# Adding the last attention norm's ln_beta to the residual rows in the first graph layer, in a late VectorE stage

## The reference, cut to what matters

```python
x = _layernorm(x + _L0_gnn_ref(x, edge_index, ...))                 # first layer: graph convolution
x = _layernorm(x + _L1_gnn_ref(x, edge_index, edge_weight1, ...))   # second layer: attention, 3 rounds
x = _layernorm(x + _L2_gnn_ref(...))
x = _layernorm(x + _L3_gnn_ref(...))

def _L1_gnn_ref(x, ...):
    x = _layer_norm(x, ln_in_g, ln_in_b)
    for l in range(3):
        h = elu(_transformer_conv(x, ...))
        x = _layer_norm(x + h, ln_g[l], ln_b[l])   # (x - mu) * rsqrt(var + eps) * g + b
    return x
```

## Time and profile before

| what | value |
|---|---|
| median of 3 runs | 7026.21 us (7023.27 to 7031.01) |
| the profiled execution's own time | 7027.23 us |
| its span in the profile | 7025.3 us |
| VectorE busy | 5733.4 us (82%) |
| TensorE busy | 4875.6 us (69%) |
| ScalarE busy | 4768.1 us (68%) |
| GpSimd busy | 4470.3 us (64%) |
| mean granted TensorE clock | 0.84 |

### The profile page before, as it was taken

The page is one execution under the profiler, slowest core; times in us unless marked ns, Lnnn a source line. Parts: engine busy times, 40 slices in busy tenths (PEclk is TensorE's granted clock), DMA queues, the critical chain, the costliest instruction groups (busy, mean ns, idle before and its releaser), DMA issues. The chain is left out here.

```text
span 7025.3 us, 129182 instructions
## 1 busy us (share of the span) xinstructions
PE 4875.6 (69%) x27083; PEld 3611.4 (51%) x27083; DVE 5733.4 (82%) x28646; ACT 4768.1 (68%) x13748; POOL 4470.3 (64%) x4380
## 2 busy tenths in 40 slices
PE   4104333332999987999948888884997659888882
PEld 1002222221877766777736666653664547666661
DVE  9814777775999987999949999995775877999996
ACT  0002888884888885888948888883553656888884
POOL 7776777772655526555537777744774445777774
PEclk8555555555999998999979999996998989999995
DMA  3333555552555534555524555544664873444441
GB/s 100 99 104 83 133 131 128 130 132 84 178 185 178 190 138 140 185 185 177 176 86 152 170 170 170 169 147 130 205 203 148 295 269 120 148 147 147 147 145 44
DMA packets 507778, 1065.66 MB, mean 152 GB/s; under 512 B 225329, under 2 KB 259196, under 8 KB 506998
## 3 DMA queue, kind: packets, MB, share of 16 engines
q1 hardware_dynamic: 373618, 811.78, 35.3%
q0 software_dynamic: 133504, 247.46, 13.2%
HBM read 559.18 MB, written 500.53 MB: 151 GB/s over the span
## 5 line engine op out<-in xcount | busy, mean ns | idle before, releaser
L1801 POOL DMA_INDIRECT xs<-tab,rec x1176 | 1187.9, 1010 | 737.0 <-issue 325.1
L1891 ACT ACTIVATE z<-p_a 128x512 f32<-128x512 f32 x1176 | 696.4, 592 | 307.1 <-PE p_a L1734 299.3
L1885 ACT ACTIVATE st<-xs,cb 128x128 f32<-128x128 f32 x2352 | 807.5, 395 | 0.5 <-DVE cg L1530 0.5
L1836 PE MATMUL p_a<-w_all,xt 128*128 128x256 f32 x2352 | 735.5, 395 | 19.9 <-ACT xt L1876 16.4
L1804 POOL DMA_INDIRECT xd<-tab,rec x616 | 621.0, 1008 | 187.8 <-issue 179.9
L1839 PE MATMUL p_y<-w_all,xt 128*128 128x258 f32 x2352 | 725.0, 390 | 21.1 <-DVE cA L1956 20.5
L1991 DVE SCALAR_TENSOR_TENSOR st<-st,cg 128x128 f32<-128x128 f32 x2352 | 711.5, 342 | 6.8 <-ACT st L1885 4.6
L1956 DVE CUSTOM_DVE_ANT_0 junk<-p_y,xs 128x129 f32<-128x129 f32 x2352 | 579.9, 283 | 53.5 <-PE p_y L1839 51.1
L1738 PE MATMUL p_m<-w_all,z 128*128 128x128 f32 x2352 | 580.0, 329 | 0.0
L999 PE MATMUL p_m<-b_rows,ones_bf 3*128 3x512 bf16 x224 | 100.1, 447 | 688.8 <-ACT z L1042 688.8
L1734 PE MATMUL p_a<-ident,st 128*128 128x128 f32 x2352 | 465.2, 280 | 145.1 <-DVE st L1991 144.9
(11 more groups left out here) (756 smaller groups left out, 16246.7 us busy)
## 6 DMA issues: line engine op xcount, KB each, us to landing
states<-st SPq DMA_DIRECT2D x168, 910.0 KB
own<-tab SPq DMA_DIRECT2D x168, 448.0 KB
tab<-o SPq DMA_DIRECT2D x168, 448.0 KB
runs<-run SPq DMA_DIRECT2D x112, 448.0 KB, 2.9
tab<-out SPq DMA_DIRECT2D x112, 448.0 KB
x<-tab SPq DMA_DIRECT2D x112, 448.0 KB, 4.3
angles<-st SPq DMA_DIRECT2D x56, 532.0 KB, 2.9
xsrc<-got SPq DMA_DIRECT2D x56, 448.0 KB
```

The costliest lines, as they stand in the source:

```text
L1801: pool.indirect_dma_start(xs[:, i, j, 0:D], None, table, bass.IndirectOffsetOnAxis(ap=rec[:, i, SRC, j : j + 1], axis=0)).then_inc(got_in[ ...
L1836: ins = pe.matmul(p_a[two(own_c, own_i)][:, 2 * D : 4 * D], xt[:, two(c, i), D : 2 * D], k.w_own[:], start=True, stop=True)
L1885: ins = act.activation(state_of(r, j)[:, h, :], xs[:, c.slot(UB), j, 0:D], ACT.Copy, scale=co.b[:, c.slot(2), h, j : j + 1])
L1891: act.activation(z[:, c.slot(RING), j, :], p_a[two(c, j)][:], ACT.Copy).then_inc(st_copied, 1)
```

## The change

The vector `ln_b[2]` is no longer added in the third attention round. The first layer adds it to the residual rows before they are stored, in a new VectorE stage `lift` with lag -3, the last one of the list. The stores of chunk n-3 wait for `lifted` and no longer for `second.applied2`; the loads still wait for `finished`. The vector is loaded once, ahead of SyncE's first load, into `last_b`. In `conv` the addition goes, and the addition of `res` stays at j = 2.

```diff
-        self.finished = sem("finished")
+        self.finished, self.storable = sem("finished"), None
...
                     c = chunk(t, u, -DRAIN)
                     if c.there:
-                        wait(sp, self.finished, c.count(1, 1), self.passed)
+                        wait(sp, self.storable or self.finished, c.count(1, 1), self.passed)
                         for i, table in enumerate(outs):
...
+        last_b, lifted, b_in = sb("last_b", [P, D]), sem("lifted"), sem("b_in")
...
+        def lift(dve, step, c):
+
+            dve.wait_ge(second.applied2, c.count(1, 1))
+            dve.tensor_tensor(R(n.o[0], c), R(n.o[0], c), every(last_b), ALU.add).then_inc(lifted, 1)
+
+        def bring_b(sp):
+            sp.dma_start(last_b[:], A["L1_gnn_ln_b"][k.L - 1].partition_broadcast(P)).then_inc(b_in, 16)
+
...
+            dve.wait_ge(b_in, 16)
 
         n.z_free = first.applied
-        n.finished = second.applied2
+        n.finished, n.storable = second.applied2, lifted
         n.run([(xs, k.xsrc)], [(own, A["x"], NODE), (where, k.info, SRC)], [k.res, k.tab[1]], lambda c: [R(summed, c)], [k.w_skip],
-              [(3, edges), (0, stats), (-1, residual), (0, first.root), (-1, second.root)],
+              [(3, edges), (0, stats), (-1, residual), (0, first.root), (-1, second.root), (-3, lift)],
...
-              [], prep=True, sp_stages=[(3, keep)], begin=begin, sp_end=kept,
+              [], prep=True, sp_stages=[(3, keep)], begin=begin, sp_end=kept, sp_begin=bring_b,
               pe_begin=side.tensor, sp_after={-4: side.bring, UB - 1: side.put_away})
...
                 norms[2].run(dve, step, z[:], o[:])
+                step(dve.tensor_tensor(z[:], z[:], last_b[:], ALU.add))
...
-            w_loads += [(k.ln_g[:], k.a["L1_gnn_ln_g"][l].partition_broadcast(P)), (k.ln_b[:], k.a["L1_gnn_ln_b"][l].partition_broadcast(P))]
+            w_loads += [(k.ln_g[:], k.a["L1_gnn_ln_g"][l].partition_broadcast(P))]
...
                     if n == 1:
-                        at["affine"] = order.put(dve.tensor_tensor(v, v, every(k.ln_b), ALU.add))
-                    elif n == 2:
                         dve.wait_ge(res_in[c.slot(2)], (c.use(2) + 1) * 16)
                         dve.tensor_tensor(v, v, res[:, c.slot(2)], ALU.add).then_inc(res_free, 1)
...
-                        if last and c4.there and j < 3:
-                            affine(j, c4)
+                        if last and c4.there and j in (0, 2):
+                            affine(j // 2, c4)
...
-                    step(dve.tensor_tensor(of[:], of[:], k.ln_b[:], ALU.add))
```

## The result

The changed kernel takes 7167.2 us (median of 4 runs, 7159.6 to 7172.6), the kernel before 7024.7 us on the same chip: ratio 1.0201, 95% interval 1.0188 to 1.0214, or +142 us. It is slower, as forecast, but by four times the forecast +35 us, and 42 us above the top of the range. The profiled execution has a span of 7165.9 us.

What follows compares the result with a forecast made beforehand. The prediction took GpSimd's gathers to bound `gcn` and VectorE the third attention round. Its terms, -50 + 74 + 8 + 3 = +35 us, gave a forecast of 7060 us, range 6992 to 7125 us.

Steps and rivals of the forecast that it cites:

- What bounds `gcn`, and the direction: In `gcn`, GpSimd's gathers bind at 18.2 us a chunk; the later record makes them wait, so the kernel gets slower.
- The attention round, -50 us: Third attention round, bound by VectorE: 56 additions of 1.00 us go, 50 us counted, bounds 10 and 56.
- `lift` and the gathers: In `gcn`, `lift` leaves the gathers' 0.94 us alone; one stretched to 1.70 us per chunk would cost 18 us.
- The loop's form, (L + D)/2 over 47 chunks: In `gcn`, the chunk period is (21.7 + 17.8)/2 = 19.8 us, 1.6 us over 18.2, costing 74 us.
- 1.58 to ScalarE's start: In `gcn`, first term of L: 1.58 us from a chunk's last gather until ScalarE starts to weigh it.
- The other terms of L: In `gcn`, from ScalarE's start to GpSimd's next gather: 13.35, 1.4, 0.2, 1.3, 3.7 and 0.2 us.
- The scaling between the two near rows: In `gcn`, the record's landing behind 896 KB of stores, scaled between 1.8 and 4.7 us: 3.7 us.
- VectorE's own part, at most 5 us: In `gcn`, the addition's 1.4 us fits VectorE's 1.68 us wait for logs, costing 0 to 0.1 us x 50.
- The smaller terms, 8 + 3 us: In `gcn`, loop-turn stops no longer hidden cost 8 us; an extra load and the stage's end cost 3 us.
- VectorE's wait for the roots: In `gcn`, VectorE's wait for ScalarE's logs, 1.68 us before, is still there and not shorter.
- The hidden record: Rival: in `gcn` the record is still early, so only 5 and 3 us are lost; 6981 us, chance 0.13.
- The landing as on an empty queue: Rival: in `gcn` the record lands in 1.8 us, L is 19.8 us; -13 us, 7013 us, chance 0.12.

Runs made afterwards that it cites:

- Wait without work: Changed kernel with `lift` only signalling and VectorE adding nothing, so `ln_b` is missing from the result: 7123.6 us, ratio 1.0135 to the kernel before.
- the store one chunk later: Changed kernel with `lift` still last and SyncE storing in the iteration after, everything computed: 6979.9 us, ratio 0.9938 to the kernel before.
- the round alone: Kernel before with only the attention round's addition left out and `gcn` unchanged: 6982.1 us, ratio 0.9931.
- the addition into the spare tile: Changed kernel with VectorE adding into a tile nobody reads and stores waiting as before the change: 6999.3 us, ratio 0.9954 to the kernel before.
- `lift` first: Changed kernel with `lift` opening VectorE's list, ahead of `edges`, everything computed: 6992.1 us, ratio 0.9939 to the kernel before.
- `runs` and `meta` late: Changed kernel with SyncE holding both until VectorE has counted the statistics of `second` in the same iteration: 7117.6 us, ratio 1.0129 to the kernel before.

## Why the prediction went wrong, point by point

- **What bounds `gcn`, and the direction: right.** GpSimd's gathers wait for `rec`, which stands behind stores that wait for `lift`. Wait without work and the store one chunk later show it from both sides.
- **The attention round, -50 us: right.** -53 us in the changed kernel, -47 us for the whole of the round alone. The reason given for the long gathers was a guess, and the traces bear it out: of 589 gathers in the round before (3800 to 4600 us) 78 last over 1.3 us, and every one of them starts while VectorE is in an instruction of over 0.9 us; in the changed kernel (4000 to 4800 us) it is 43 of 612, again every one.
- **`lift` and the gathers.** Nor did `lift` lengthen the gathers of `gcn`: 25 long ones of 669, before 37 of 668, and the means are 994 and 986 ns, before 995 and 980. But the inference that the prediction quotes, that a `tensor_tensor` leaves the writing of descriptors alone, is not what these traces show: 32 of those 37 start inside a `tensor_tensor` of 1.1 us, and none of the 573 that start outside VectorE's long instructions is long. No run isolates it.
- **The loop's form, (L + D)/2 over 47 chunks: right.** Its chain is in the changed trace, link by link, and 47 chunks at the measured 22.05 us are 181 of the 189 us. That the sum of the terms read there gives 22.3 us is no further proof, since it must nearly do so.
- **The step that failed is the term "1.58 to ScalarE's start".** It was taken from the earlier trace rows as a fixed latency of the gathers. In the binding chunk it is 7.1 us, of which 6.96 are the gathers' landing: 5.5/2 x 47 = +130 us, more than the whole miss in `gcn` (189 against 85). The prediction moved the stores to behind `lift`, and left unasked what else goes out at that time. `edges`, which starts as `lift` ends, releases `runs` and `meta`, so all of SyncE's traffic joins in one burst beside the gathers. I looked at the earlier trace rows, where small pieces of `meta` made a record late, and set it aside with "those pieces are not ahead of it here". They are not ahead of the record, but beside the gathers. And the trace of the kernel before had the lateness already, in a chunk's first gathers (5.7 us), where it cost nothing; the change moved it to the last ones.
- **The other terms of L.** Roots 13.35 us (13.35 forecast), `lift` 1.4 (1.4), SyncE 0.2 (0.2), stores to record 1.15 (1.3). From the record's issue to GpSimd 3.6 us against 3.9 with the 0.2 us behind the landing; the landing itself is 2.9 us in the median, just under the forecast 3 to 5:

```profile
DMA to landing us min/median/max: 2.7/2.9/5.3
```

  The scaling between the two near rows made the landing 0.8 us too long, and the ring rule of the Trainium skill ("DMA: Bandwidth & Descriptors", "Queues, rings and completion order") points the right way: on an empty queue the same record landed in 1.8 us.
- **VectorE's own part, at most 5 us: open.** 14.5 us with the addition into the spare tile, 5 us with `lift` first, nothing with the store one chunk later, and traces of an unchanged `gcn` differ by 5 us. Why the first of these is over 5 us was not followed.
- **The smaller terms, 8 + 3 us: not shown.** Outside the 181 us of the loop the stage has 8 us more than before, and no run takes them apart.
- **VectorE's wait for the roots: right.** It is there and longer, 9.02 us in the iteration shown, since ScalarE, too, starts late.
- **The rivals.** The hidden record is what the changed kernel is not, and what it becomes with the store one chunk later: -49 us, where that rival had -45 (its terms, +8 in `gcn` and -50 to -56 in the round, were about -5 and -55). The landing as on an empty queue would have been too good by 1.1 us. None of them, and not the range, held a longer gather end. Its bounds had the landing free and left L's first term fixed.

Still open: what in the burst holds the gathers' landing. The pieces of `meta` are some 3 of the 5.5 us. The packets in the changed kernel's trace fit this: those of 4 KB that carry gathered rows take 0.84 to 1.05 us each when they start within 3 us of the last 4-byte piece, and 0.21 us over the stage (medians, from 700 to 1600 us). For the rest the stores, the record and `xsrc` could not be taken apart. The somewhat longer gathers in the kernel with `runs` and `meta` late are not explained either.

## What to carry to other kernels

Before a wait is added to a queue that also loads, follow the load that is queued behind it into the loop in which it takes part, and write down which transfers will now start together, and beside what: a term of that loop that was a short latency when the queue was quiet (1.6 us here) can become the largest change of it (7.1 us). Look in the trace for the same burst where it does no harm, since its price can be read there (5.7 us here, on a chunk's first gathers). A late step at the end of an engine's list can release its store one iteration later, when the buffers allow it; here that turned +142 us into -49 us with two edited lines. And an instruction moved from a full engine stage to one with slack gives nearly its whole length (53 of 56 us), if its wait stays out of the loops.

## What the runs showed of the hardware that I had not expected

- The landing of indirect gathers goes with what the SyncE queue has in flight. Behind the end of a chunk's last gather it takes 1.4 us with the queue quiet, 3.1 to 3.35 us beside two stores, a record and a load, 4.1 us with `runs` added, and 7.0 us with the 4-byte pieces of `meta` too (medians of the binding chunks).
- Packets being through is not the landing: in the burst read above the last 3584-byte packet of the four big transfers ended at 1251.6 us, and `runs` reported its landing at 1254.64, within half a microsecond of `meta` and of the gathers.
- Size says little of a landing: the `meta` store of 3.5 KB in 4-byte pieces takes 6.9 us before and 8.0 in the burst (medians), the `runs` store of 448 KB takes 2.9 and 6.8, and 2.6 when it is moved out of the burst.
- Some chips run this program 25% slower (8750 to 8842 against 7028 to 7037 us), with gaps ahead of VectorE's instructions; there the change that costs 2% elsewhere can't be seen.
